# Sums of squares of the first attention's queries: a product with one column of ones in place of 128

## What is computed

```python
q = (layernorm(x) @ Wq).reshape(B, Sq, H, D)      # B*Sq = 1024 rows, H = 16 heads, D = 128
k = (ctx @ Wk).reshape(B, Skv, H, D)
v = (ctx @ Wv).reshape(B, Skv, H, D)
q = q * rsqrt(mean(square(q), axis=-1) + eps) * gq
k = k * rsqrt(mean(square(k), axis=-1) + eps) * gk
out = softmax(einsum('bqhd,bkhd->bhqk', q, k) / sqrt(D)) @ v
x = x + out.reshape(B, Sq, H * D) @ Wo
```

## Time and profile before

| | us |
|---|---|
| median of 3 runs | 1029.34 |
| lowest and highest | 1029.27, 1031.43 |
| the profiled execution's own time | 1028.96 |
| its span, first to last instruction | 1027.4 |
| PE, PEld busy in it | 867.6, 615.1 |
| DVE, ACT, POOL busy in it | 708.8, 535.8, 448.0 |
| mean granted TensorE clock | 0.922 of full |

### The profile page before, as it was taken

How to read it: one execution, slowest core, us unless ns; L and a number is a source line. 1 busy time by engine, 2 the same in 40 slices (tenths; PEclk the granted TensorE clock), 3 DMA queues, 4 the chain that set the end, 5 groups by cost and what they waited for, 6 DMA issues and landing times.

```text
span 1027.4 us, 13071 instructions
## 1 busy us (share of the span) xinstructions
PE 867.6 (84%) x4348; PEld 615.1 (60%) x4352; DVE 708.8 (69%) x1367; ACT 535.8 (52%) x991; POOL 448.0 (44%) x274
## 2 busy tenths in 40 slices
PE   5795899999999999645579986858688799999998
PEld 3354777777877777513354643728577685545646
DVE  4247689999899998778848566765989863353311
ACT  2486687787778778733313442535678472112120
POOL 1211678777778886556810002007458540600000
PEclk8898899999999999866879998958699899999999
DMA  4003000100000100000520000000000001100000
GB/s 126 16 5 133 16 17 16 31 15 15 15 15 15 31 3 6 1 0 1 198 83 0 1 1 1 1 0 1 2 1 2 1 1 48 83 0 1 12 9 21
DMA packets 12924, 24.25 MB, mean 24 GB/s; under 512 B 4280, under 2 KB 8656, under 8 KB 11728
## 3 DMA queue, kind: packets, MB, share of 16 engines
q1 hardware_dynamic: 12448, 20.53, 6.2%
q10 hardware_dynamic: 432, 3.15, 0.8%
HBM read 22.63 MB, written 1.05 MB: 23 GB/s over the span
## 4 chain that ended last, share of the span: by engine, by line
PE 30%; DVE 14%; issue 4%; ACT 4%; POOL 1%; ACTq 0%; DVEq 0%
PE PS L2131 12%; PE PS L2180 6%; PE PS L2234 3%; DVE mxf L1574 2%; DVE regD L1612 1%; PE PS L2035 1%; PE PS L1674 1%; DVE regB L1612 1%; PE PS L2011 1%; PE PS L2198 1%; PE PS L2049 1%; PE PS L2218 1%; PE PS L2219 1%; DVE xn L1051 1%; PE PS L2083 1%
## 5 line engine op out<-in xcount | busy, mean ns | idle before, releaser
L487 POOL TENSOR_TENSOR X<-X,xn 128x512 f32<-128x512 f32 x62 | 103.4, 1668 | 69.1 <-ACT xn L712 68.6
L454 POOL TENSOR_SCALAR veps<-mv 128x4 f32<-128x4 f32 x16 | 3.6, 228 | 265.9 <-DVE mv L1042 265.8
L1141 DVE TENSOR_TENSOR_SCAN regB<-regB 128x1024 f32<-128x1024 f32 x32 | 85.5, 2671 | 0.2
L1122 DVE TENSOR_SCALAR_CACHE_REDUCE regA<-PS,nrq 128x256 bf16<-128x256 f32 x128 | 56.0, 475 | 38.2 <-PE PS L1749 36.3
L731 ACT ACTIVATE regA<-PS,nb,rq 128x256 f32<-128x256 f32 x128 | 72.1, 576 | 11.7 <-DVE regA L1122 10.9
L2234 PE MATMUL PS<-regA 128*128 128x128 f32 x512 | 74.8, 293 | 3.4 <-ACT regA L994 3.3
L480 POOL TENSOR_TENSOR y<-y,regB 128x1024 f32<-128x1024 f32 x32 | 75.7, 2364 | 3.5 <-DVE regB L1152 3.4
L1771 PE MATMUL PS<-regA 128*128 128x256 f32 x256 | 67.0, 384 | 7.3 <-DVE qss L1109 7.2
L2234 PEld LDWEIGHTS PS<-regA 128*128 128x128 f32 x512 | 68.2, 206 | 7.1 <-ACT regA L994 6.1
L1749 PE MATMUL PS<-regA 128*128 128x256 f32 x256 | 67.1, 385 | 0.0
L1780 PE MATMUL PS<-regA 128*128 128x256 f32 x256 | 66.5, 383 | 0.0
(11 more groups left out here) (276 smaller groups left out, 2162.6 us busy)
## 6 DMA issues: line engine op xcount, KB each, us to landing
regA<-in_W SPq DMA_DIRECT2D x16, 384.0 KB, 3.0
regB<-in_wg SPq DMA_DIRECT2D x2, 1024.0 KB, 6.5
regB<-in_wu SPq DMA_DIRECT2D x2, 1024.0 KB, 8.5
X<-in_x SPq DMA_DIRECT2D x1, 1024.0 KB, 8.2
regC<-in_wg ACTq DMA_DIRECT2D x1, 1024.0 KB, 5.8
regC<-in_wu ACTq DMA_DIRECT2D x1, 1024.0 KB, 8.0
regC<-in_wd ACTq DMA_DIRECT2D x1, 1024.0 KB, 10.0
regB<-in_wd SPq DMA_DIRECT2D x1, 1024.0 KB, 9.9
```

The lines of the kernel that those rows point to most:

```text
L487: pool.tensor_tensor(xt, xt, part, ALU.add).then_inc(x0_add, 1)
L1122: ins = dve.tensor_scalar(spill[:, i, q, :], bank(S_BANK + i)[:, q * S:(q + 1) * S], nrq[par][:, t:t + 1], None, ALU.mult, ALU.min, accum_ ...
L1141: dve.tensor_tensor_scan(v(hs), v(dA), v(dBu), 0.0, ALU.mult, ALU.add).then_inc(scan_done, 1)
```

## The change

The moving operand of the eight products of each head becomes one column of `ones` instead of 128, and the output one column of PSUM instead of 128. The number of instructions, their order, the stationary operands, all waits and what VectorE reads stay as they are.

```diff
                 pe.wait_ge(qsq_done, h + 1)
                 for t in range(NT):
-                    last = pe.matmul(to[:, t:t + P], sq[:, t * P:(t + 1) * P], ones[:, :], start=True, stop=True)
+                    last = pe.matmul(to[:, t:t + 1], sq[:, t * P:(t + 1) * P], ones[:, 0:1], start=True, stop=True)
                 last.then_inc(ss_mm, 1)
```

## The result

| | before | after |
|---|---|---|
| median of 20 runs | 1030.83 us | 1032.46 us |
| lowest and highest | 1029.27, 1032.34 | 1030.25, 1036.02 |
| profiled execution, its span | 1028.96, 1027.4 | 1031.69, 1030.1 |
| mean granted clock in it | 0.922 | 0.919 |

The ratio is 1.0019, with a 95% interval from 1.001 to 1.0028: the change makes the kernel slower, by 1.6 us by the two medians and by 2.0 us by the ratio. The forecast was no change, 1029.1 us, from 1027.3 to 1031.0. The time lies outside that range. About 1.5 us of the distance is the kernel before itself, whose median over 20 runs is 1030.83 where the three runs shown had 1029.34; the rest, 1.9 us, is a loss that the forecast had not put where it is.

What follows compares the result with a forecast made beforehand. VectorE's chain was taken to bound the loop, with L1742 beside it; 0.14 us from head 0 and 0.1 from heads 1, 2 and 15 gave 0.2 of 1028.96, plus 0.4 for the runs' median: 1029.1 us, range 1027.3 to 1031.0.

Steps and rivals of the forecast that it cites:

- What bounds the loop: Heads 3 to 14: VectorE's path to L1103 bounds; TensorE's L1734 waits 12 times, 5.0 us; L1742 lies beside it.
- the slack read from the rows: Loop heads: L1742 has 0.25 or 0.58 us to spare beside VectorE's path.
- The pace of the row: L1742's 16 products in each head: weight loads set the spacing, going from 0.111 to 0.109 us, 0.03 us gained per head.
- My lower bound of 0.06 us: Lowest possible pace of L1742's loads, read from L1734's first two loads, 0.20 - 0.14 = 0.06 us apart.
- Head 0: Head 0, where VectorE idles 7.43 us for L1742's result: gain of 0.03 + 0.11 = 0.14 us.
- the clock falls: Slower rival: one-column products leave the array little to stream, the clock falls in each loop head, 17 us lost, 1046; chance 0.04.
- The sum: All heads: 0.14 us in head 0, 0.03 each in heads 1, 2 and 15, none in 3 to 14; 0.2 us in all.
- the forecast case: Whole kernel: gain of 0 to 0.6 us, with other waits shifting by a few tenths; chance 0.86.
- around each L1742 TensorE is packed: Argument against the falling clock in loop heads: TensorE has dense work around every row of L1742.
- 1.05 + 0.77 = 1.8 us: Loss of two groups of four products after idle time from 98 to 105 us: 2.08 and 1.80 us, 1.03 at full clock.
- within 0.2%: Whole kernel: a difference of about 0.2%, 2.1 us, can be told from no change; same 0.86, faster 0.07, slower 0.07.

Runs made afterwards that it cites:

- the bf16 kernel: Squares written as bf16 and multiplied with 128 columns of bf16 ones in heads 3 to 15, against the kernel before: 1029.48 us, ratio 0.999.

## Why the prediction was wrong, point by point

*What bounds the loop: right.* Twelve waits of L1734, 5.0 us before and after; with the row shortened by 1.34 us the waits took it all up, and with the row doubled each head lost 1.48 us where the slack read from the rows gave 1.37.

*The pace of the row: right.* The moving columns do not set it. I took 0.109 us from the loads' growth with their columns; measured 0.112, so the row gained nothing rather than 0.03. That it is the load that sets it is the reading left over, since no run changed the loads' columns; an issue of one instruction need not take as long, since the eight bf16 pairs took 0.45 us, 0.056 each. My lower bound of 0.06 us came from the first two of L1734's loads; all eight take 0.86 us, so they are (0.86 - 0.14) / 7 = 0.103 apart, and the whole row shows no pace as low as the bound. The Trainium skill's page "TensorE: Matmul & The Clock Gate" gives about 60 cycles, some 25 ns, for products of 1 to 64 columns (section "Back-to-back issue gap"). The same section calls this the gap of a product by itself and says that in a stream of loads and products both set the spacing, a limit that the prediction left out. These pairs come 112 ns apart with one column, so the 25 ns does not carry over to them. That page's rule for LDWEIGHTS, columns over 1.2 (section "LDWEIGHTS (loading the stationary operand)"), gives an estimated 107 ns, and the measured 112 is near it.

*Head 0: right.* Its result was expected 0.14 us earlier. From the row's start to L1109 were 34.33 - 32.27 = 2.06 us before; after it is 35.71 - 33.76 = 1.95:

```profile
35.71 0.17 DVE L1109 TENSOR_SCALAR qss<-PS 128x8 f32<-128x8 f32 x1 [8.55 <-PE PS L1742]
```

*The rival "the clock falls": right mechanism, wrong place, and so mis-sized in chance and in price.* This is the step that failed. I weighed it for the loop, at 0.04 and 17 us, and there it does not happen: the clock stayed at 1.00 from 120 to 400 us, with TensorE busy for 274.9 of 280 us, and even in the bf16 kernel, where it is busy for 258.4. That the dense work around the rows holds it there is my reading and was not tested by itself. I had written that the rival decides "from the point where two heads or so lose it", and I did not ask the same question of heads 0, 1 and 2. The sum gave heads 1 and 2 a gain of 0.03 us each and no loss, and the forecast case put "a fall of the clock in the first 110 us landing elsewhere" at a few tenths of a us: measured is a new fall behind head 1's row, with 1.5 us. Nor is "around each L1742 TensorE is packed" a sign of safety: from 44 to 60 us, ahead of head 1's row, TensorE was busy for 15.2 of 16 us before, and still the columns of this row decided. I even used head 0 as evidence against the rival, since its row of 128-column products ran at full speed behind 2.25 us of idle time: but those columns are what the change takes away, and with one column the half-clock stretch behind that row comes some 3 us earlier. Rows of the kernel before can't speak for what an instruction does to the clock once its columns are gone. A fall in one head, with a price of 1.05 + 0.77 = 1.8 us read from the earlier trace rows, would have been a rival with 1030.9 us and a fair chance. Its price was nearly right: 1.5 in the table.

*The sum and the range.* Of the gain of 0.2 us the traces show head 0's 0.11; against it stands a loss of 1.6 to 2.0. The range rested on three runs of before; 20 runs put its median 1.5 us higher. With that shift the forecast would have been 1030.6 and its range would have ended near 1032.5, just beyond the measured 1032.46: the number would then have fallen inside by luck, with the loss as unforeseen as before. The centre of the range stood on too few runs.

*The size: "within 0.2%".* The measured 0.19% lies just inside that bound, but its interval excludes no change.

What stays open: why the time behind head 15 differs between traces of kernels that are alike there (634.8 to 638.2 us). Half-clock stretches lie in it whose starts, counted from head 15, differ by up to 1.6 us from trace to trace; that they make the difference was not tested. Heads 0 and 2 cost nothing by themselves (0.9994 with 128 columns in head 1 alone); whether they add to the loss once head 1 falls is open, since the difference between 1.0011 and 1.0015 to 1.0019 is within the intervals. Three of the 20 runs of after took 1035.7 to 1036.0 us, 2 us more than any other; none of the 11 further runs of the same kernel did, and no trace is of such a run.

## What to carry to other kernels

Before you shorten what TensorE streams, look at the loads: here f32 products with a new stationary operand of 128 columns each came 0.112 us apart with 128 moving columns and with one, and fewer moving columns gave nothing. Then ask, for each place where the line runs and not for the loop alone, what the columns did for the clock; columns that compute nothing useful may be what keeps TensorE at full speed there, as in head 1. And where idle stretches lower the clock ahead of work on the path, useless products in them can pay: here 5.7 us for a few lines.

## What the runs showed of the hardware that I had not expected

TensorE's busy record and what holds its clock up are two things. Behind head 1's row, from 64 to 70 us, the record is packed in both kernels, 5.45 and 6.00 of 6 us, and the granted clock is 1.00 in one and 0.50 in the other. With 16 loads at the same pace until the clock falls, 128 or 64 columns in head 1's row left the clock at 1.00, and 32 or 1 let it fall to the lower level. These are observations of this row in its surroundings, and no limit for another place. The Trainium skill's page "TensorE: Matmul & The Clock Gate" (section "What's actually happening") says that the throttled clock is the default and that activity releases it; what these runs add, for this place, is that a row of loads with products of 32 columns or one did not hold the clock, though its record is as busy as that of a row with 128.

The falls are not independent. In the five traces of the table with the fall at 61 to 71 us the one at 81 to 85 is missing (it is missing in the one with 64 columns too, which is the quickest from head 1 to head 3), the stretch around 100 to 112 us moves with it, and the net price of the first, 1.5 us, is about half of the 2.8 us that it cost where the other idle stretches were filled. That the missing second fall and the moved third one are what gives the difference back is argued from the rows, not tested by themselves.
